# Reading a Strassen kernel's PSUM banks two at a time

## What is computed

```python
# x: (64, 64, 1024), itok_B_0_15: (64,), L0_cond_weights: (16, 64, 64)
W = weights[condition]
xf = einsum('bct,bcd->bdt', x, W).reshape(4096, 1024)
scores = xf @ Wr.T                       # 64 experts
top_vals, top_idx = top_k(scores, 16)
gates = softmax(top_vals)
G = zeros((N, 64)).at[arange(N)[:, None], top_idx].set(gates)
h = einsum('nd,krd->nkr', xf, A)         # 64 experts x rank 16 = 1024
out = einsum('nkr,kdr->nd', h * G[:, :, None], B)
result = x + 2.0 * out
```

## Time and profile before

| | |
|---|---|
| median of 3 runs | 715.27 us (715.18 to 715.5) |
| the profiled execution | 715.55 us |
| its span, first to last instruction | 713.8 us |
| granted TensorE clock, mean | 1.000 |
| TensorE busy | 708.6 us (99%), 3414 matmuls |
| VectorE busy | 477.6 us (67%), 924 instructions |
| ScalarE busy | 254.2 us (36%), 483 instructions |
| DMA | 178.46 MB, mean 250 GB/s |

### The profile page before, as it was taken

One profiled execution on the slowest core, in us unless ns is written; L12 is line 12 of the kernel. 1 busy time (PEld: TensorE's weight loads), 2 busy tenths in 40 slices (PEclk: granted clock), 3 DMA queues, 4 the chain that ended last, 5 costly groups with the idle time before them and its releaser, 6 DMA issues.

```text
span 713.8 us, 9927 instructions
## 1 busy us (share of the span) xinstructions
PE 708.6 (99%) x3414; PEld 596.2 (84%) x3414; DVE 477.6 (67%) x924; ACT 254.2 (36%) x483; POOL 1.6 (0%) x6
## 2 busy tenths in 40 slices
PE   8999999999999999999999999999999999999998
PEld 8888888888888888888888888888888888888886
DVE  5898999995538686755342868774544396778542
ACT  5675553525326431223322552132223264213200
POOL 0000000000000000000000000000000000000000
PEclk9999999999999999999999999999999999999999
DMA  9976679746886758466667774755767787546653
GB/s 327 406 294 279 215 283 395 280 195 247 300 294 245 291 183 293 164 221 239 240 244 279 274 287 147 280 198 191 291 210 262 253 310 254 186 146 201 228 222 145
DMA packets 56691, 178.46 MB, mean 250 GB/s; under 512 B 9666, under 2 KB 10818, under 8 KB 56130
## 3 DMA queue, kind: packets, MB, share of 16 engines
q1 hardware_dynamic: 54722, 174.29, 67.7%
q10 hardware_dynamic: 1920, 3.54, 1.4%
HBM read 131.66 MB, written 46.14 MB: 249 GB/s over the span
## 4 chain that ended last, share of the span: by engine, by line
PE 98%; DMA 1%; ACTq 0%; DVE 0%; issue 0%
PE Pb L481 43%; PE Pb L448 42%; PE Cb L430 8%; PE S L491 4%; DMA BR<-in_x 1%; PE T L545 0%; PE T L539 0%; PE Pb L464 0%; PE T L505 0%; PE S L505 0%; DVE Q L747 0%; ACTq L296 0%; ACTq L632 0%
## 5 line engine op out<-in xcount | busy, mean ns | idle before, releaser
L448 PE MATMUL Pb<-Op,Wt 128*128 128x512 f32 x996 | 235.0, 392 | 0.0
L448 PEld LDWEIGHTS Pb<-Op,Wt 128*128 128x128 f32 x996 | 185.6, 188 | 37.8
L481 PE MATMUL Pb<-Wt,Op 128*128 128x512 f32 x912 | 212.3, 391 | 0.0
L481 PEld LDWEIGHTS Pb<-Wt,Op 128*128 128x128 f32 x912 | 170.1, 188 | 34.8 <-DVE Op L747 0.4
L747 DVE TENSOR_TENSOR Q<-Pb,Q 128x512 f32<-128x512 f32 x112 | 77.4, 691 | 88.6 <-PE Pb L481 88.4
L481 PE MATMUL Pb<-Wt,Ox 128*128 128x512 f32 x432 | 100.8, 391 | 0.0
L481 PEld LDWEIGHTS Pb<-Wt,Ox 128*128 128x128 f32 x432 | 80.6, 188 | 16.2
L591 ACT COPY R<-Cb 128x512 f32<-128x512 f32 x60 | 35.1, 587 | 147.0 <-PE Cb L430 147.0
L747 DVE TENSOR_TENSOR Cq<-Pb,Cq 128x512 f32<-128x512 f32 x64 | 44.0, 688 | 51.4 <-ACT Cq L715 32.2
L747 DVE TENSOR_TENSOR Op<-R,Op 128x512 fp32r<-128x512 f32 x98 | 64.7, 685 | 19.1 <-ACT Op L576 19.1
L448 PE MATMUL Pb<-Ox,Wt 128*128 128x512 f32 x288 | 66.3, 390 | 0.0
(11 more groups left out here) (84 smaller groups left out, 404.8 us busy)
## 6 DMA issues: line engine op xcount, KB each, us to landing
Wt<-Wd SPq DMA_DIRECT2D x168, 512.0 KB, 4.8
Wd<-Wt SPq DMA_DIRECT2D x56, 512.0 KB, 4.7
Q<-in_x SPq DMA_DIRECT2D x32, 512.0 KB, 5.1
xc<-in_x SPq DMA_DIRECT2D x24, 512.0 KB, 3.9
out<-Q SPq DMA_DIRECT2D x32, 256.0 KB, 2.6
out<-Q SPq DMA_DIRECT2D x16, 512.0 KB, 2.7
BR<-in_B SPq DMA_DIRECT2D x3, 1024.0 KB, 8.3
BR<-in_x SPq DMA_DIRECT2D x8, 256.0 KB, 11.2
```

The source lines that it names most:

```text
L448: t = e.matmul(Pb[:, j, :], Wt[:, k, a, 128 * c:128 * c + 128], part((USES1[m], s, c), z), start=fresh and (c, a, z) == (0, 0, 0), stop=(c ...
L481: t = e.matmul(Pb[:, i, :], part((USES2[m], s, c), a)[:, 128 * i:128 * i + 128], Wt[:, k, z, :], start=fresh and (c, a, z) == (0, 0, 0), s ...
```

## The change

ScalarE's copies and VectorE's adds read the tiles from PSUM in pairs: nothing is done at tiles 0 and 2, and at tiles 1 and 3 one instruction of 128 x 1024 reads banks 0 and 1, or 2 and 3. The semaphore is raised by 2 when the instruction ends. In the very last block product (round 3, Q3) the tiles are still read one by one. TensorE's queue and its waits are not changed, nor are SyncE's.

```diff
-                        if name in a_prod:
+                        if name in a_prod and j % 2:
                             e.wait_ge(p_first, tile_done(s, m, j))
...
-                            e.copy(Cq[:, {"P2": 1, "P1": 0, "P5": 3, "P3": 2}[name], j, :], Pb[:, j, :]
-                                   ).then_inc(a_prod[name], 1)
+                            e.copy(Cq[:, {"P2": 1, "P1": 0, "P5": 3, "P3": 2}[name], j - 1:j + 1, :],
+                                   Pb[:, j - 1:j + 1, :]).then_inc(a_prod[name], 2)
...
-            def add(to, one, two, on, op=ALU.add):
-                e.tensor_tensor(to, one, two, op).then_inc(on, 1)
+            def add(to, one, two, on, op=ALU.add, n=1):
+                e.tensor_tensor(to, one, two, op).then_inc(on, n)
...
             def drain_first(s, m, j):
-                name, P = FIRST[m], Pb[:, j, :]
+
+                name, P = FIRST[m], Pb[:, j - 1:j + 1, :]
+                if j % 2 == 0:
+                    return
                 if name == "P1":
                     e.wait_ge(a_prod["P1"], 4 * s + j + 1)
                     e.wait_ge(a_prod["P2"], 4 * s + j + 1)
-                    add(Cq[:, 1, j, :], P, Cq[:, 1, j, :], v_prod["P1"])
+                    add(Cq[:, 1, j - 1:j + 1, :], P, Cq[:, 1, j - 1:j + 1, :], v_prod["P1"], n=2)
                 elif name in v_prod:
...
-                    add(Cq[:, q, j, :], P, Cq[:, q, j, :], v_prod[name])
+                    add(Cq[:, q, j - 1:j + 1, :], P, Cq[:, q, j - 1:j + 1, :], v_prod[name], n=2)
 
             def drain_second(s, m, i):
                 name = SECOND[m]
+
+                n = 1 if (s, m) == (NS - 1, 6) else 2
+                if i % n != n - 1:
+                    return
                 tile, half = INTO[name][0] + i, INTO[name][1]
-                to = Q[:, tile, 512 * half:512 * half + 512]
+                to = Q[:, tile + 1 - n:tile + 1, 512 * half:512 * half + 512]
...
-                add(to, Pb[:, i, :], to, v_out)
+                add(to, Pb[:, i + 1 - n:i + 1, :], to, v_out, n=n)
```

## The result

The changed kernel takes 718.57 us (median of 5, 717.08 to 719.46) where the kernel before takes 715.50 (5, 715.18 to 715.57): ratio 1.0039, 95% interval 1.0028 to 1.0051, so 3.1 us or 0.4% slower, with a scatter of 2.4 us where these five of the kernel before have 0.4. The forecast was 717.2, between 715.0 and 718.2. The sign and the place were right, the size was not.

A forecast was written before the change was run, and what follows sets the result against it. TensorE's stream was taken as the bound. A 2.24 us loss at P7's first tile less 0.29 regained at 108 us gave +1.95, say +1.9, on a median of 715.27: 717.2 us, range 715.0 to 718.2.

The forecast's parts named there:

- The bound: Whole kernel: TensorE's stream bounds it, busy 99% of the span; changed bank reads cannot shorten it, save a 0.4 us wait.
- 5.2 us: VectorE in all: 86 pairs each save 0.06 us by next starts, 5.2 us together, off the path.
- the list of signs: Profile after: one new TensorE wait of about 2.3 us near 84 us, none near 108, VectorE busy 0 to 5 us lower.
- The place: P6 in round 0: VectorE is in backlog, so P7's first matmul waits for bank 0, freed only with bank 1.
- The size of the gap: P7's first tile, round 0: pair starts 84.79, takes 1.22, weight load goes 2.33 us later; TensorE loses 2.24.
- The interference of rounds 1 to 3: P1's pair in rounds 1 to 3 ends at 226.8, wanted at 228.15: 1.4 us to spare, so no wait.
- the 4.19 us: P6, round 0: between its first two adds VectorE does 4.19 us of other work: splits and the last top-16 steps.
- TensorE waits 0.4 us for VectorE in all: Whole kernel: argument against VectorE's saving reaching the clock, since TensorE's waits for VectorE total only 0.4 us.
- The wait at 108 us: TensorE's old 0.4 us wait for the fourth G12 split goes: a gain of 0.29 us, with 0.5 to spare.
- What was late next: P6's second pair, round 0: starts 89.41, ends 90.6; P7's third tile wants bank 2 at about 91.9, spare 1.2 us.
- TensorE loses 2.24 us: P7's first tile, round 0: load 2.33 us later, about 0.10 caught up; bounds 1.80 to 2.44.
- rival D: Second stall at P7's bank 2 or P1's pairs, or clock falls behind the gap: +3 to +6, 718.3 to 721; chance 0.13.

The follow-up runs named there:

- the second occasion: The changed kernel run once more, unaltered, against the kernel before: 719.24 us, ratio 1.0049.
- The short gap: Changed kernel with round 0's last top-16 steps moved behind the P6 pair, against the kernel before: 716.41 us, ratio 1.0011.
- the gap of 5.32 us: Changed kernel with six more VectorE operations ahead of the P6 pair, against the kernel before: 722.33 us, ratio 1.0095.

## Why the prediction was right and wrong

- **The bound, and what can't be gained.** Right. VectorE was busy 10.5 us less and ScalarE 4.1, and none of it reached the time, but for the 0.3 at 108 us. VectorE's busy time fell by more than forecast (5.2 us, and 0 to 5 in the list of signs): the busy time of the profile counts the 0.69 us of an instruction that starts after an idle moment in full, and where VectorE waits for each tile, two singles are 1.38 and a pair 1.22; 5.2 us is the price by next starts, in backlog.
- **The place.** Right: P6's first pair in round 0, which alone gives a loss and without which there is none.
- **The size of the gap.** Right at full clock, link by link: ScalarE's pair 1.02, the start at 84.79, 1.22 long, the load 2.33 late, 2.25 lost. The interference of rounds 1 to 3: none, as forecast. One reading on the way was off without moving the sum: the 4.19 us between the starts of P6's two adds hold the first add's own 0.60, so VectorE's other work between them is 3.59. And "TensorE waits 0.4 us for VectorE in all" leaves out the start, where the same view has 0.7 us for `wbd`.
- **The wait at 108 us.** Right, 0.30 won back (5.44 for 5.74).
- **What was late next.** P7's third tile, with 1.2 us to spare, was the right place: in the changed kernel's profile the pair starts at 88.98+0.42 = 89.40, forecast 89.41, and nothing waits; it broke as soon as the first gap was shortened.
- **The step that failed** is "TensorE loses 2.24 us", as the whole price of the gap. It priced the idle time at the full clock, and left what TensorE does after it to rival D, together with unrelated mishaps, at a chance of 0.13. D began at 718.3, outside the range, though the prediction says that the range holds its start. By their mean clock the fall comes in 6 of the 10 executions of the changed kernel, and its price is 1.59 us in the profile that has it. Even as a rival it was mis-sized: D priced a slow tile at 2.7, all twelve matmuls at the lower clock; 1.59/0.227 is seven of them, and the windows show the clock at 0.50 for a part of the tile only. With the fall the sum is 1.95+1.59 = 3.54 above the kernel before, and the profiled execution shows 3.53. The evidence against a fall was thin: the trace of before has no gap of this length in TensorE's work, so that a clock of 1.00 in every window said nothing about it. A cost unknown in this way belonged in the upper bound: 717.2+1.6 alone is above the 718.2 of the range.
- **The median of the first five, 718.57**, is itself an execution without a fall by its clock of 1.000. It is in the middle because two with a fall lie above it; on the second occasion, with four of five, the middle one has the fall. The four without a fall average 718.09 and the six with one 719.24. What else lifted 718.57 above the 717.5 of an execution at full clock stays open. A later start is one candidate: the sum took the start as in the profile before, 41.39, and it was seen as late as 42.25, 0.9 us more, though on another chip.
- **The short gap's expectation** failed at another step: of work that is moved behind one reader, the next reader in the queue pays.

## What to carry to other kernels

Merging two reads of PSUM into one instruction saves 0.06 us of VectorE and holds the first bank until the second tile is read: look for the boundary at which the reader is in backlog, and price it there, since one such place costs more than all others save. A gap in a stream of matmuls is worth its length plus a possible fall of the clock behind it, here 1.6 us in 6 of 10 executions for a gap of 2.4; where the gap can't be avoided, a few useless matmuls within it can be cheaper than the fall. Scatter that appears with a change can hide a term that one profiled execution does not show; look at the mean clock of each (0.998 here; 0.999 stands in executions of the kernel before too). Before two profiled executions are compared, take off what their starts differ by: here that alone is up to 1.3 us, and with it off the sums close to 0.02 us.

## What the runs showed of the hardware

With the gap of 2.36 us the clock stood at 1.00 during the gap and was lower only when the work had begun again (0.62 and 0.53 in the two windows of 2 us behind it); with the gap of 5.32 us it fell shortly before the work began (0.69 from 88.5 to 89.0, work from 89.04). So a clock of 1.00 within a gap doesn't clear it: the windows behind it have to be read too. Two executions of one program with the same gap, 2.37 and 2.36 us, differ in whether it falls. One instruction over two PSUM banks costs what one over 1024 SBUF columns does: 1.22 us on VectorE, and 1.02 on ScalarE, 0.84 ns a column more than the 512 form.
